# Graph attention layer on Trainium2: where the unused gather places point

## The chip, the cores and the metric

The kernel runs on one core of one Trainium2 chip (trn2). The metric is the device time of one execution in microseconds (us). TensorE is called PE here, its weight loads PEld, VectorE DVE, ScalarE ACT, GpSimd POOL and SyncE SP; ACTq, SPq and POOLq are their DMA queues.

## The reference

A relation-aware graph attention layer with a residual and a layer norm. There are N = 6250 nodes of 256 channels, E = 100000 edges sorted by their destination, and R = 5 relations with 4 heads of 64 channels:

```python
Q = (einsum('nc,rch->rnh', x, Wq) + bq).reshape(R, N, HEADS, OUT)   # K and V alike
q_i, k_j, v_j = Q[edge_type, dst], K[edge_type, src], V[edge_type, src]
score = sum(q_i * k_j, axis=-1) * scale
seg = dst * R + edge_type
e = exp(score - segment_max(score, seg)[seg]);  alpha = e / segment_sum(e, seg)[seg]
out = segment_sum(v_j * alpha, dst) + bias
return layernorm(x + out)
```

## The kernel before

**Three stages.** From 0 to about 322 us DVE sorts the edges while PE projects the queries: each of NT = 49 tiles of 128 nodes gives QC = 3 chunks of queries, NOQ = 147 in all, which go to the table `q_tab` in HBM (31250 rows of 256 float32, 1 KB each; the row of node n and relation r is 5n + r). From 322 to about 810 us PE projects keys and values, 5 chunks of 512 columns a tile, 245 in all (line 633), into four PSUM banks. DVE adds the bias to each (line 1168) and writes it to one of two stage buffers; the ACT queue stores a whole tile of 1280 KB from there to `kv_tab` (line 796; 31250 rows of 512 float32, 2 KB each). From about 811 to 1920 us the edges are worked off in 208 steps of four tiles of 128 edge places. Then come the sums across pieces and the layer norm.

**Slots of nodes.** Besides the 100000 edges, the sorted list has one extra entry for each of 49 x 128 = 6272 node numbers, so that every node occurs. `real` is 1 for an edge and 0 for such a slot. The 831 tiles in use (USED) hold 106368 places, so 6368 of them, 7.66 a tile, are no edges; the last 96 are padding. `kvidx` has for every place the row of `kv_tab` that POOL gathers (line 468), one indirect DMA for each tile of 128 places, 256 KB; the row is `lof * real` (line 1029), where `lof` is relation times N plus source. `nodef` is the node of the place. What a slot fetches is not used further.

**The block list.** Edges with the same destination and relation share one query row. While PE projects keys and values, POOL gathers query rows in sorted order from `q_tab` (line 450) and SP writes them to a second table, `q_seg` (line 506). The sorted edges lie in 128 rows of F = 1024 places, one a partition, of which ROWS = 104 are in use; the distinct segments of each row are packed in blocks of RB = 32. `seg_tab` in HBM holds their q_tab rows, 32 blocks for each row. There are BLK x 128 = 9 x 128 = 1152 places for blocks. Function `ranks` (lines 1095 to 1144) works out which block of `seg_tab` each place takes and writes it to `blk_i` (line 1143), for partition p and column b the place 128 b + p; POOL reads the blocks into `seg_list` by nine indirect DMAs (line 438), and then issues NQ = 288 gathers, each of 128 rows of 1 KB: gather j takes column j of `seg_list`, which is entry j mod 32 of the 128 blocks of column j div 32.

With the inputs of the reference, counted on the host, 984 of the 1152 places hold a block: columns 0 to 6 wholly, column 7 in partitions 0 to 87, column 8 in none. A place without a block takes a row of `seg_tab` of partition 127, where every entry is 0. So the gathers j = 224 to 255 fetch row 0 of `q_tab` in 40 of 128 partitions, and j = 256 to 287 in all 128. The blocks in use hold 30022 segments; their other 1466 entries are 0 as well, in both kernels.

**Order and rings.** A gather of query rows writes one of PQ = 13 buffers and waits until the write to `q_seg` from that buffer 13 gathers before has landed; from j = 73 on it also waits for a number of evicted chunks (function `done_chunks`, EASE = 72). The eviction of the first chunk of a tile waits until the store from its stage buffer two tiles before has landed (line 1166). PE waits for the eviction four chunks before. The first gather of `kv_tab` waits for all of these writes. In the third stage POOL runs up to KL = 5 steps of gathers ahead of DVE's products (line 1201), and a ring of KS = 22 steps ties it to PE's sums (line 697).

**Where DVE works out the indices.** After the sort DVE runs `ranks` in one piece, then steps 0 to 3 of `indices` (line 1029 is step 3), and only then starts to evict (lines 1162 and 1168). The wrapper `c(...)` waits for each instruction before the next is issued; `c.go(...)` doesn't.

Of the kernel before, what the change touches and what calls it, by code (L numbers as in the profile page):

```python
# [5 lines left out]
P = 128  # L6


def gnn_kernel(nc, x, src, dst, etype, Wq, bq, Wk, bk, Wv, bv, bias, out):
    f32, i32, u16, bf16 = mybir.dt.float32, mybir.dt.int32, mybir.dt.uint16, mybir.dt.bfloat16  # L10
    ALU, ACT, AX = mybir.AluOpType, mybir.ActivationFunctionType, mybir.AxisListType
# [23 lines left out]
    F = 1024  # L35
# [35 lines left out]
    RB = 32  # L71
    ROWS = -(-USED // FH)
# [73 lines left out]
    with ctx:  # L146
        def sb(name, shape, dt=f32):
            return ctx.enter_context(nc.sbuf_tensor(name, shape, dt))

        def sem(name):  # L150
            return ctx.enter_context(nc.semaphore(name))
# [5 lines left out]
        part_f = sb("part_f", [P, 1])  # L157
        kvidx = sb("kvidx", [P, TT], i32)
# [20 lines left out]
        def cut(words):  # L179
            nonlocal top  # L180
            top += words
            assert top <= REGION, top
            return region[:, top - words:top]
# [13 lines left out]
        lof, real, segi_w, is_head, is_tail = cut(TT), cut(TT), cut(TT), cut(TT), cut(TT)  # L197
# [15 lines left out]
        seg_list, blk_i = cut(NQ).bitcast(i32), cut(BLK).bitcast(i32)  # L213
# [3 lines left out]
        nodef = other[:, 0:TT]  # L217
# [10 lines left out]
        nblk, b32 = st0[:, 2 * F + 2 * P:2 * F + 2 * P + 1], st0[:, 2 * F + 2 * P + 1:2 * F + 2 * P + 2]  # L228
        cmp32 = st0[:, 2 * F + 2 * P + 8:2 * F + 2 * P + 8 + RB]
        below = st0[:, 0:BLK * P].rearrange("p (b n) -> p b n", b=BLK)  # L230
        bval, bcnt, bmax = (pqf[:, 3 * F + 16 * u:3 * F + 16 * u + BLK] for u in range(3))
# [66 lines left out]
        s_ranks, s_nblk, s_prefix, s_blocks = sem("s_ranks"), sem("s_nblk"), sem("s_prefix"), sem("s_blocks")  # L298
# [654 lines left out]
        def _(dve):  # L953
            c = Chain(dve, s_dve)
# [20 lines left out]
                                                op0=ALU.mult, op1=ALU.add))  # L975
# [34 lines left out]
            def indices(step):  # L1010
# [12 lines left out]
                if step == 2:  # L1023
# [2 lines left out]
                    c(nc.vector.scalar_tensor_tensor(out=lof[:], in0=nrel[:], scalar=-float(SRCS - N), in1=lof[:],  # L1026
                                                     op0=ALU.mult, op1=ALU.add))
                if step == 3:
                    c(nc.vector.tensor_tensor(kvidx[:], lof[:], real[:], ALU.mult))
                if step == 4:  # L1030

                    nc.vector.tensor_scalar(nodef[:], nodef[:], float(P * NT), None, ALU.min).then_inc(s_node, 1)
# [4 lines left out]
                if step == 7:  # L1037
                    dve.wait_ge(s_cast, 1)
                    c.go(nc.vector.scalar_tensor_tensor(out=rel[:, 0:512], in0=bank[5][:], scalar=float(N0MAX),
                                                        in1=nodef[:, 0:512], op0=ALU.min, op1=ALU.subtract))  # L1040
                    c.go(nc.vector.scalar_tensor_tensor(out=rel[:, 512:TT], in0=bank[6][:, 0:TT - 512],
                                                        scalar=float(N0MAX), in1=nodef[:, 512:TT], op0=ALU.min,
                                                        op1=ALU.subtract))
# [18 lines left out]
                if step == 10:  # L1062
# [4 lines left out]
                                                     in1=nrel[:, 0:NCK], op0=ALU.add, op1=ALU.mult))  # L1067
# [9 lines left out]
                if step == 13:  # L1077

                    c(nc.vector.scalar_tensor_tensor(out=nrel[:], in0=rel[:], scalar=1.0, in1=real[:],
                                                     op0=ALU.subtract, op1=ALU.mult))  # L1080
                    c(nc.vector.tensor_scalar(nrel[:], nrel[:], -1.0, -1.0, ALU.mult, ALU.add))
                if step == 14:

                    c(nc.vector.scalar_tensor_tensor(out=nrel[:], in0=is_head[:], scalar=float(P + 2), in1=nrel[:],
                                                     op0=ALU.mult, op1=ALU.add))
                    c(nc.vector.scalar_tensor_tensor(out=nrel[:], in0=is_tail[:], scalar=float(P + 3), in1=nrel[:],
                                                     op0=ALU.mult, op1=ALU.add))
# [7 lines left out]
            def ranks():  # L1095
# [16 lines left out]
                                               in0=cum.rearrange("p (f n) -> p f n", n=P), scalar=1.0,  # L1112
                                               in1=base_l.unsqueeze(2).broadcast_to([P, FH, P]), op0=ALU.subtract,
                                               op1=ALU.subtract).then_inc(s_ranks, 1)
                c(nc.vector.scalar_tensor_tensor(out=word[:], in0=seg_r[:], scalar=10, in1=place[:],
                                                 op0=ALU.logical_shift_left, op1=ALU.bitwise_or))
# [3 lines left out]
                for k in range(10):  # L1120
# [8 lines left out]
                                                 op0=ALU.mult, op1=ALU.add))  # L1129
# [10 lines left out]
                c(nc.vector.tensor_tensor(bval[:], bval[:], bmax[:], ALU.subtract))  # L1140
                c(nc.vector.scalar_tensor_tensor(out=bval[:], in0=bcnt[:], scalar=float(F // RB), in1=bval[:],
                                                 op0=ALU.mult, op1=ALU.add))
                nc.vector.tensor_scalar(blk_i[:], bval[:], float(F // RB), float(P * F // RB - 1), ALU.subtract, ALU.min
                                        ).then_inc(s_blocks, 1)

            for e in range(len(NET)):
                sort_entry(e)
            dve.wait_ge(s_sort, len(NET))
            ranks()
            for step in range(4):  # L1150
                indices(step)
            dve.wait_ge(s_b, 16 * 2 * R)
            dve.wait_ge(s_bq, 16 * R)
            for o in range(OS, NO):
                t, c0, w = chunk(o)
                n = nodes(t)
                if OA <= o < NOQ:
                    if o % QC == 0:
                        dve.wait_ge(s_qout[t % 2], 16 * (t // 2))
                    dve.wait_ge(s_proj, o + 1)  # L1160
                    q0 = c0 - 2 * R * C
                    nc.vector.tensor_tensor(stage_q[0:n, t % 2, q0:q0 + w], bank[o % 4][0:n, 0:w],
                                            bq_sb[0:n, q0:q0 + w], ALU.add).then_inc(s_evD, 1)
                if o >= NOQ:
                    if t >= 2 and c0 == 0:
                        dve.wait_ge(s_kvout[t % 2], 16 * (t // 2))
                    dve.wait_ge(s_proj, o + 1)
                    nc.vector.tensor_tensor(stage[0:n, t % 2, c0:c0 + w], bank[o % 4][0:n, 0:w],  # L1168
                                            b_sb[0:n, c0:c0 + w], ALU.add).then_inc(s_evD, 1)
                if o >= Z + 4:  # L1170
                    indices(o - Z)
# [258 lines left out]
```

## Time and profile before

| | us |
|---|---|
| median of 3 runs | 2065.13 (2061.58 to 2067.93) |
| profiled execution, its own time | 2069.55 |
| its span, first to last instruction | 2067.7 |
| DVE busy | 1617.8 (78%) |
| PE busy | 1689.1 (82%) |
| POOL busy | 1150.7 (56%) |

The profiled execution is taken by the hardware profiler. Busy time leaves out register, branch, semaphore and DMA-issuing instructions, but counts POOL's work on an indirect DMA. In the slices, each digit is the busy share of one fortieth of the span (51.7 us), in tenths, 9 for 90% or more; PEclk is the granted PE clock in tenths of full speed, DMA the busy share of the 16 DMA engines, and GB/s what they moved. A DMA's landing time runs from its issue until its data is there. The granted clock has two levels, 2.4 GHz (1.00) and 1.2 GHz (0.50).

### The profile page before, as it was taken

What the parts mean: (1) busy time and instruction counts of PE and PEld (TensorE: products, weight loads), DVE (VectorE), ACT (ScalarE), POOL (GpSimd) and SP (SyncE); (2) the same over time, 40 slices, a digit from 0 to 9 for tenths busy, and PEclk for the clock granted to TensorE, in tenths of its full rate; (3) what the DMA queues carried; (4) which work ended last, traced back from release to release, by engine and by line L of the source; (5) the groups of instructions that cost most, each with busy time, mean ns of one, the idle gap of its engine ahead of it and who ended that gap; (6) DMA issues with size and microseconds to landing.
All of it is one profiled execution on the core that took longest, in us unless ns stands there. A gap on an engine that the chain in (4) does not pass through costs nothing.

```text
span 2067.7 us, 33198 instructions
## 1 busy us (share of the span) xinstructions
PE 1689.1 (82%) x7565; PEld 1132.7 (55%) x7565; DVE 1617.8 (78%) x4144; ACT 1045.3 (51%) x4107; POOL 1150.7 (56%) x1215
## 2 busy tenths in 40 slices
PE   6999999999999497578877878778877888777545
PEld 2444444444444143466766766667666776666543
DVE  7988897354443143789999999999999999999648
ACT  1223230200000000078888888878888788878845
POOL 2000005777777302777777777777777777776104
PEclk9999999999999798789999999999999999999879
DMA  6333336999999965999999999999999999999006
GB/s 211 123 122 122 117 132 203 317 359 364 364 362 320 175 198 204 349 325 322 330 328 323 313 335 319 326 312 315 334 334 313 306 320 335 331 317 308 24 22 207
DMA packets 339496, 555.34 MB, mean 269 GB/s; under 512 B 44045, under 2 KB 238831, under 8 KB 339298
## 3 DMA queue, kind: packets, MB, share of 16 engines
q0 software_dynamic: 80880, 256.60, 38.2%
q1 hardware_dynamic: 222180, 228.67, 33.9%
q10 hardware_dynamic: 36238, 67.94, 9.0%
q8 instruction: 61, 1.00, 0.2%
q14 instruction: 137, 1.12, 0.2%
HBM read 412.09 MB, written 140.94 MB: 267 GB/s over the span
## 4 chain that ended last, share of the span: by engine, by line
DVE 40%; PE 29%; issue 17%; DMA 6%; POOL 4%; DVEq 3%; ACT 1%; SPq 0%; ACTq 0%; POOLq 0%
PE sums L633 23%; DVE region L1258 6%; DVE region L996 6%; DVE region L1201 5%; POOL region L468 4%; DVE region L1190 4%; DVE acc L1284 3%; DMA kv_tab<-region 3%; PE pairs L709 3%; PE sums L697 2%; DVE region L1267 2%; DMA region<-kv_tab,kvidx 2%; DVEq L1275 2%; DVE region L1212 1%; DVE region L1250 1%
## 5 line engine op out<-in xcount | busy, mean ns | idle before, releaser
L468 POOL DMA_INDIRECT region<-kv_tab,kvidx x831 | 818.3, 985 | 360.3 <-issue 213.0
L633 PE MATMUL sums<-region,acc 128*128 128x512 f32 (+2 forms) x1568 | 683.4, 582 | 32.0 <-DVE region L1168 31.7
L881 ACT ACTIVATE region<-region 128x64 f32<-128x64 f32 x2496 | 694.6, 352 | 0.0
L709 PE MATMUL pairs<-region 128*128 128x256 f32 x1664 | 450.7, 418 | 175.8 <-DVE region L1201 157.6
L633 PEld LDWEIGHTS sums<-region,acc 128*128 128x128 f32 (+1 forms) x1568 | 286.4, 191 | 336.4 <-issue 292.2
L709 PEld LDWEIGHTS pairs<-region 128*128 128x128 f32 x1664 | 324.1, 205 | 252.1 <-issue 197.5
L697 PE MATMUL sums<-region 128*128 128x131 f32 x3328 | 433.2, 284 | 27.9 <-issue 24.5
L697 PEld LDWEIGHTS sums<-region 128*128 128x128 f32 x3328 | 412.7, 197 | 57.7 <-issue 44.8
L1168 DVE TENSOR_TENSOR region<-sums,region 128x512 f32<-128x512 f32 (+1 forms) x245 | 168.3, 691 | 286.9 <-PE sums L633 239.4
L450 POOL DMA_INDIRECT region<-q_tab,region x288 | 274.5, 953 | 122.0 <-issue 58.9
L899 ACT COPY acc<-sums 128x256 f32 x832 | 305.8, 368 | 29.7 <-PE sums L697 28.3
L1201 DVE TENSOR_TENSOR region<-region,pairs 128x512 f32<-128x512 f32 x416 | 278.5, 677 | 32.6 <-DMA region<-kv_tab,kvidx 21.4
L1207 DVE TENSOR_REDUCE region<-region 128x16 f32<-128x1024 f32 x208 | 252.3, 1213 | 0.6 <-issue 0.2
L868 ACT COPY region<-bank 128x128 f32<-128x128 f32 x26 | 6.9, 265 | 460.8 <-PE bank L679 460.6
L1258 DVE TENSOR_SCALAR region<-iota_f,nrel 128x131 f32<-128x131 f32 x832 | 195.9, 313 | 10.3 <-PE sums L697 10.3
L996 DVE TENSOR_TENSOR region<-region 128x512 f32<-128x512 f32 x292 | 189.0, 689 | 5.1
L787 ACT COPY region<-sums 128x512 f32<-128x512 f32 x138 | 71.0, 514 | 210.2 <-PE sums L633 210.2
L1284 DVE TENSOR_TENSOR acc<-acc,region 128x2 f32 x832 | 130.9, 157 | 31.6 <-ACT region L907 10.8
L430 POOL DMA_DIRECT2D rel_tab<-region x1 | 0.8, 766 | 245.7 <-DVE region L1111 245.7
L1190 DVE TENSOR_SCALAR region<-region,part_f 128x512 f32<-128x512 bf16 x208 | 102.3, 492 | 10.2 <-DMA region<-rel_tab 10.2
L477 POOL TENSOR_TENSOR region<-region 128x256 f32<-128x256 f32 (+1 forms) x49 | 35.4, 731 | 113.8 <-DMA region<-in_x 113.5
L1267 DVE TENSOR_TENSOR region<-region 128x256 f32<-128x256 f32 x208 | 87.0, 418 | 0.0
(239 smaller groups left out, 943.6 us busy)
## 6 DMA issues: line engine op xcount, KB each, us to landing
region<-q_seg SPq DMA_DIRECT2D x832, 128.0 KB
kv_tab<-region ACTq DMA_DIRECT2D x48, 1280.0 KB, 7.8
q_seg<-region SPq DMA_DIRECT2D x288, 128.0 KB, 5.7
q_tab<-region SPq DMA_DIRECT2D x48, 640.0 KB, 3.3
region<-rel_tab SPq DMA_DIRECT2D x208, 128.0 KB, 5.2
region<-kv_tab,kvidx POOLq DMA_INDIRECT x831
region<-in_x SPq DMA_DIRECT2D x96, 128.0 KB, 3.2
out<-region SPq DMA_DIRECT2D x48, 128.0 KB, 2.5
```

What stands on the lines that cost most here:

```text
L450: pool.indirect_dma_start(pq[:, j % PQ, :], None, q_tab, bass.IndirectOffsetOnAxis(ap=seg_list[:, j:j + 1], axis=0)).then_inc(s_pq[j % PQ] ...
L468: pool.indirect_dma_start(ring_row[:, a:a + 2 * C], None, kv_tab, bass.IndirectOffsetOnAxis(ap=kvidx[:, t:t + 1], axis=0)).then_inc(s_got[ ...
L633: done = nc.tensor.matmul(bank[o % 4][0:n, 0:w], acc[:, k, t * P:t * P + n], w_sb[:, k, :, :].rearrange("p u c -> p (u c)")[:, c0:c0 + w], ...
L697: done = nc.tensor.matmul(bank[i][:, h * W:(h + 1) * W], ring_v[:, i, spot(q), h * P:(h + 1) * P], oneh[:, q % 2, i, :], start=True, stop= ...
L709: done = nc.tensor.matmul(qk[:, i, :], oht[:, s % 2, i * P:(i + 1) * P], qring[:, s % QS, i, :], start=True, stop=True)
L881: done = nc.scalar.activation(ring_v[:, i, spot(q), h * D:(h + 1) * D], ring_v[:, i, spot(q), h * D:(h + 1) * D], ACT.Copy, scale=alT[:, h ...
L899: nc.scalar.copy(acc[:, :, bass.ds(at[(q % 2) * SB + i] + 1, P)], bank[i][:, 0:2 * W].rearrange("p (h n) -> p h n", h=2)[:, :, 0:P]).then_ ...
L996: nc.vector.tensor_tensor(to[:, :, half, :], one, other_half, ALU.max if half else ALU.min).then_inc(s_sort, 1)
L1201: nc.vector.tensor_tensor(prod[:, two, :], ring_k[:, two, spot(s), :], qk[:, two, :], ALU.mult).then_inc(s_mul, 1)
L1207: nc.vector.tensor_reduce(sc[:, (s // PERC) % 2, :, g:g + SB].rearrange("p h g -> p g h"), prod.rearrange("p i (h d) -> p i h d", h=H), AX ...
L1258: done = nc.vector.tensor_scalar(oneh[:, q % 2, i, :], iota_f[:, 1:W + 1], nrel[:, t:t + 1], None, ALU.is_equal)
L1284: nc.vector.tensor_tensor(acc[:, :, bass.ds(col, 1)], acc[:, :, bass.ds(col, 1)], cols[:, q % CS, i, :, 2:3], ALU.add).then_inc(s_acc, 1)
```

## The change

Three places. In step 3 of `indices` the row gathered by a slot becomes the number of its node in place of 0: kvidx = (lof - nodef) * real + nodef, two more DVE operations on 128 x 832. In `ranks` a place without a block takes a block by its partition: the first block of row p for p < 104, the second block of row p - 104 for the others. For that `blk_i` is worked out by six small DVE operations instead of one. `b32` and `bcnt` are buffers that are free at that point.

```diff
                 if step == 3:
-                    c(nc.vector.tensor_tensor(kvidx[:], lof[:], real[:], ALU.mult))
+                    c(nc.vector.tensor_tensor(lof[:], lof[:], nodef[:], ALU.subtract))
+                    c(nc.vector.tensor_tensor(lof[:], lof[:], real[:], ALU.mult))
+                    c(nc.vector.tensor_tensor(kvidx[:], lof[:], nodef[:], ALU.add))
...
-                nc.vector.tensor_scalar(blk_i[:], bval[:], float(F // RB), float(P * F // RB - 1), ALU.subtract, ALU.min
-                                        ).then_inc(s_blocks, 1)
+
+                per = F // RB
+                c(nc.vector.tensor_scalar(b32[:], part_f[:, 0:1], float(ROWS), 1.0 - ROWS * per, ALU.is_ge, ALU.mult))
+                c(nc.vector.scalar_tensor_tensor(out=b32[:], in0=part_f[:, 0:1], scalar=float(per), in1=b32[:],
+                                                 op0=ALU.mult, op1=ALU.add))
+                c.go(nc.vector.tensor_scalar(bcnt[:], bval[:], float((ROWS + 1) * per), None, ALU.is_lt))
+                c(nc.vector.tensor_scalar(bval[:], bval[:], float(per), b32[:, 0:1], ALU.subtract, ALU.subtract))
+                c(nc.vector.tensor_tensor(bval[:], bval[:], bcnt[:], ALU.mult))
+                nc.vector.tensor_scalar(blk_i[:], bval[:], b32[:, 0:1], None, ALU.add).then_inc(s_blocks, 1)
```

## Rows read from the trace of the kernel before

**Rows 1.** The profile's page: the span in 40 slices.

```profile
PE   6999999999999497578877878778877888777545
DVE  7988897354443143789999999999999999999648
PEclk9999999999999798789999999999999999999879
DMA  6333336999999965999999999999999999999006
GB/s 211 123 122 122 117 132 203 317 359 364 364 362 320 175 198 204 349 325 322 330 328 323 313 335 319 326 312 315 334 334 313 306 320 335 331 317 308 24 22 207
```

**Rows 2.** Chain of waits that ended last, 650 to 910 us: start, length, what.

```profile
649.98 8.60 PE sums L633 x20
658.60 0.70 DVE region L1168
659.32 28.55 DMA kv_tab<-region
687.90 0.70 DVE region L1168
688.65 3.80 PE sums L633 x4
692.47 0.70 DVE region L1168
693.19 30.77 DMA kv_tab<-region
723.98 0.70 DVE region L1168
724.72 82.33 PE sums L633 x184
807.07 0.70 DVE region L1168
```

**Rows 3.** Busy time by stretch: length, PE, PEld, DVE, ACT, POOL (x), PEclk, DMA share, GB/s.

```profile
424.83:658.58 233.75, 233.75 (x545) 103.89 (x546) 95.09 (x138) 0.00 (x0) 176.76 (x188) 1.00 1.03 363
658.58:688.65 30.07, 15.44 (x37) 6.49 (x36) 4.80 (x8) 0.00 (x0) 12.20 (x13) 0.80 1.02 189
706.30:724.72 18.42, 2.13 (x5) 0.58 (x4) 0.74 (x2) 0.00 (x0) 2.83 (x3) 0.61 1.02 167
```

**Rows 4.** POOL's instructions in order of time: start, length, what, idle before and releaser.

```profile
656.01 0.94 POOL L450 DMA_INDIRECT region<-q_tab,region  x1 [0.30 <-DVE region L1168]
...
658.51 0.95 POOL L450 DMA_INDIRECT region<-q_tab,region  x1 [0.30 <-DMA q_seg<-region]
659.76 0.95 POOL L450 DMA_INDIRECT region<-q_tab,region  x1 [0.30 <-issue]
...
675.97 0.94 POOL L450 DMA_INDIRECT region<-q_tab,region  x1 [5.12 <-DMA q_seg<-region]
...
728.37 0.95 POOL L450 DMA_INDIRECT region<-q_tab,region  x1 [0.30 <-issue]
```

**Rows 5.** Line 796 (stores to kv_tab), landing: started 500 to 550, then 615 to 655 us.

```profile
DMA to landing us min/median/max: 7.2/7.6/8.1
DMA to landing us min/median/max: 8.7/8.8/8.9
```

**Rows 6.** Line 450 (query gathers), landing: 500 to 550, 615 to 655, 658.6 to 690 us.

```profile
DMA to landing us min/median/max: 3.7/5.1/6.7
DMA to landing us min/median/max: 3.9/5.9/7.0
DMA to landing us min/median/max: 6.0/11.7/15.7
```

**Rows 7.** Line 1168 after 659.5 us: count, min/median/max ns, first and last start.

```profile
L1168 DVE TENSOR_TENSOR region<-sums,region x65: 680/691/693, 661.6 to 807.1; 128x512 f32<-128x512 f32 x60, 106x512 f32<-106x512 f32 x5
```

**Rows 8.** DVE's instructions in order of time, 315 to 322 us.

```profile
315.25 0.17 DVE L1140 TENSOR_TENSOR region<-region 128x9 f32<-128x9 f32 x1
315.45 0.17 DVE L1141 SCALAR_TENSOR_TENSOR region<-region 128x9 f32<-128x9 f32 x1
315.66 0.17 DVE L1143 TENSOR_SCALAR region<-region 128x9 int32<-128x9 f32 x1
315.74 0.59 DVE L1015 TENSOR_SCALAR region<-region 128x832 f32<-128x832 uint16 x1
...
319.63 1.02 DVE L1026 SCALAR_TENSOR_TENSOR region<-nrel,region 128x832 f32<-128x832 f32 x1
320.69 1.03 DVE L1029 TENSOR_TENSOR kvidx<-region 128x832 int32<-128x832 f32 x1
321.75 2.22 DVE L1162 TENSOR_TENSOR region<-sums,region 128x512 f32<-128x512 f32 x4
```

**Rows 9.** PE's instructions in order of time, 322 us.

```profile
322.49 12.29 PE L633 MATMUL sums<-region,acc 128*128 128x512 f32 x32 [0.23 <-DVE region L1162]
```

**Rows 10.** DVE's waits, 811 to 1920 us: total, times, longest.

```profile
DVE region L1201 <- DMA region<-kv_tab,kvidx: 21.4, 17, 3.0
DVE region L1201 <- issue: 11.2, 24, 0.5
```

**Rows 11.** Busy time 905 to 1907 us, columns as in group 3.

```profile
905.00:1907.00 1002.00, 796.31 (x4850) 680.17 (x4849) 967.59 (x2923) 820.53 (x3415) 746.37 (x757) 0.96 0.97 323
```

## The prediction

> **What bounds the kernel now.** I read the page's slices first, then the chain of waits, then busy time by stretch, and last the instructions and landing times of the lines that the chain names. The slices [rows 1] show three stages. DVE is the fullest engine at the start (the sort), PE from about slice 8, DVE again from about slice 19. One thing breaks the pattern: in slice 13, counted from 0, the DMA engines are as busy as before, but what they move falls from 360 to 175 GB/s, and PE's digit drops to 4. The chain [rows 2] shows what that costs. Up to 658.6 us it is PE's matmuls back to back. Then it runs twice through a store to kv_tab, 28.55 and 30.77 us long, and only from 724.72 us through matmuls again. A store of the same size lands in 7.6 us earlier on [rows 5]. By stretch [rows 3], PE is busy for all of 233.75 us before, for 15.44 of 30.07 us in the first of the two waits, and for 2.13 of 18.42 us at the end of the second; the DMA share stays at 1.02 while the rate falls from 363 to 189 and 167 GB/s.
>
> **What the engines do in that time.** POOL's instructions give the date [rows 4]. The last of the 288 query gathers starts at 728.37 us; 34 stand from 656.01 us on in that view, so gather j = 256, the first one that reads row 0 in all 128 partitions, is the one at 658.51 us. The slow store starts 0.8 us later. Stores, q_seg writes and gathers have not changed in kind or size at that point; only the row that is read has. Gathers land after a median of 11.7 us instead of 5.1 [rows 6], POOL finds its ring of 13 buffers full and waits 5.12 us for one [rows 4], and the stores on another queue land late with them. Column 7, where 40 of 128 partitions read row 0, is the mild form: gathers 5.9 us, stores 8.8 us [rows 5, 6], and PE doesn't stop. So row 0 gives out a limited flow: 32 gathers of 128 KB in the 69.9 us from 658.51 to 728.37 us are 60 GB/s, an estimate of that limit. Column 7 asks for 40 KB every 1.25 us (the spacing in rows 4), 33 GB/s, under it.
>
> The Trainium skill, DMA: Bandwidth & Descriptors, section Issuing engines are not separate DMA queues, states that DMAs of all issuing engines run on the same 16 DMA engines and interleave. The trace agrees, with its store of 28.55 us beside gathers of another queue.
>
> **Part 1: the places of the block list, what is removed.** With 128 different rows in the gathers 256 to 287 I expect them to run as the ones before. POOL issues them 1.25 us apart, so the last starts at 658.5 + 31 x 1.25 = 697 us, and PE goes on without a stop. One chunk takes 233.75 / 545 x 4 = 1.716 us [rows 3] (four matmul records a chunk). After the eviction at 658.60 us there are 65 more [rows 7], so the last one would start at 658.60 + 65 x 1.716 = 770.1 us instead of 807.07 us [rows 2]: **-37.0 us**. This holds the two stalls as well as the half clock after them: the four matmuls at 688.65 us take 3.80 us, 0.95 us each for 0.43 before. What is late next is nothing but PE itself, at its full clock. The cover is thin, though: a stage buffer is wanted again 8.6 us after its store starts (5 chunks x 1.716), the stores took 8.8 us in column 7 [rows 5], and four banks of PSUM give PE a few us beyond that. Bounds of the gain: 37.0 from above by PE's rate; from below see the first rival.
>
> **Part 2: six small operations for one.** The last small operations of ranks are 0.20 us apart, an operation that isn't waited for costs 0.08 us (315.66 to 315.74) [rows 8]. Five are added, four waited for: 4 x 0.20 + 0.08 = **+0.9 us**. Behind them on DVE stand the index steps and the first evictions; POOL waits for blk_i and starts its gathers 0.9 us later, which is covered, as they end more than 70 us before the projections do.
>
> **Part 3: two operations on 128 x 832.** From one to the next it is 1.06 us (319.63, 320.69, 321.75) [rows 8]: **+2.1 us**. These are not covered. DVE's first eviction at 321.75 us ends PE's wait at 322.49 us [rows 9]: PE had filled its four banks and stood for 0.23 us. Everything from there to 658 us is PE at its rate or DVE's index steps, so the 3.0 us of parts 2 and 3 go into the end one for one. The bounds are 2.5 (some wait further on eats a part) and 3.5.
>
> **Part 4: the slots' rows in kv_tab.** The trace shows no gather of kv_tab without its 7.66 rows of 128 that are row 0, so this is bounded. A tile of 128 takes about 1002 / 757 = 1.32 us [rows 11], so row 0 is asked for 7.66 x 2 KB, about 12 GB/s: well under column 7's 33 GB/s, which cost a gather 0.8 us of landing and no engine anything. From above, DVE waits 21.4 + 11.2 = 32.6 us in all at the products that need these gathers [rows 10]; more can't come back. From below, DVE is busy 967.59 of 1002 us [rows 11], and earlier data that DVE isn't waiting for is worth nothing, 0; rows near each other could also be 1 or 2 us worse. I take 12/33 of 0.8 us, 0.3 us, at some three landings that stand on the chain while the ring fills: **-1.0 us**, nearest the column 7 row.
>
> **The sum.** -37.0 + 0.9 + 2.1 - 1.0 = -35.0 us. Against the profiled execution, 2069.55 - 35.0 = 2034.6 us. That execution was 4.4 us above the median of the runs, so against the median 2065.13 - 35.0 = 2030.1 us, which I round to 2030.
>
> **Rival 1: the bus is full without the hot row too.** The DMA engines are at 1.03 before the stall [rows 3] and the stores have under 1 us to spare. If the four or five stores from 658 to 697 us land after 15 us instead of 8.8, DVE waits over 6 us each, PE some 3, so about 15 us of the 37 stay: 2030 + 15 = 2045. For it speaks the 8.8 us; against it, that this itself comes with row 0 in column 7 and that 233.75 us went by at the same load without a stop. 8 in 100.
>
> **Rival 2: the third stage gains too.** If reads of row 0 hold up the DMA engines at 12 GB/s already, half of the 32.6 us [rows 10] returns: 2030 - 16 + 1 = 2015. For it: the DMA share is 0.97 at only 323 GB/s there [rows 11], against 363 before. Against it: DVE is busy 96.6% of that stretch, and column 7 stood 33 GB/s. 7 in 100.
>
> **Rival 3: row 0 isn't the cause, or the places still lead to it.** Then the stall stays and only the operations are added: 2065.1 + 3.0 = 2068, 0.15% above. Against it is the date of the stall to 1 us. 3 in 100.
>
> **Rival 4, slower.** The new rows lie at an even distance: partition p reads the start of row p of 104, so neighbours are about 31250 / 104 = 300 rows of 1 KB, some 308 KB, apart, and the gathers of columns 7 and 8 all have that pattern, while in use neighbouring places are some 30 rows apart. If such rows shared one part of the memory and were given out at half row 0's rate, the stall would be twice as long: 2065.1 + 3.0 + 37.0 = 2105. It decides from the point where gathers take longer than the 11.7 us of row 0 [rows 6]. No row shows this distance; that the starts scatter by several rows speaks against it, as does that each address is another. 3 in 100.
>
> The Trainium skill, DMA: Bandwidth & Descriptors, section Latency and other measured facts, has a rule against this change: copies whose partitions lie 512 KiB to 8 MiB apart, by powers of two, ran at 207 down to 103 GB/s, and a pitch padded by 4 KiB at full rate. No run here shows such a pitch; 308 KB with scatter is no power of two, so by the page too the full rate is likelier, and its 103 GB/s would be a case of this rival.
>
> **From the cases to the numbers.** The forecast has 79 in 100: 2030, with its own range 2022 to 2038 (the median's spread of 3 us, the 2.5 to 3.5, two or three us in stage three). I stretch it to 2018 below and 2043 above to take in the near parts of rivals 1 and 2. A measurement of this kernel can tell about 0.3%, 6 us, from no change. Faster: 79 + 8 + 7 = 94. Same: 3. Slower: 3.
>
> **What would show it.** Right: in the changed profile DMA GB/s stays near 360 to about 700 us, the chain has no store to kv_tab of over 10 us, the last eviction at line 1168 starts near 773 us, gathers of line 450 land after about 5 to 6 us to the end with 1.25 us between them, and the first eviction starts near 324.8 us. From the last eviction to the end it takes as long as before, to within 3 us. Wrong: a stall at gather 256 that remains (rival 3 or 4), stores of 12 us and more from 658 to 697 us (rival 1), or fewer waits at line 1201 and a third stage over 10 us shorter (rival 2).

## The result and the profile after

| | before | after |
|---|---|---|
| median, us | 2066.02 (4 runs) | 2041.23 (4 runs, 2034.3 to 2043.67) |
| profiled execution, us | 2069.55 | 2043.67 |

The ratio is 0.9881, 95% interval 0.9855 to 0.9907: 24.8 us by the medians. A second comparison on one chip (experiment 1) gave 0.986, interval 0.984 to 0.9881, which is 29 us. I had said 2030 and 35 us. The measured time lies in the stated range of 2018 to 2043, but above the 2022 to 2038 that the forecast had for itself; only the stretch for the near parts of rivals 1 and 2 takes it in.

The slices of the page after, which answer to [rows 1]:

```profile
PE   5999999999999995687788877788777887788645
DVE  7988897454443344799999999999999999999548
PEclk9999999999999997899999999999999999989668
DMA  6333344999999948999999999999999999998006
GB/s 214 124 124 109 124 141 160 313 350 364 364 362 363 339 154 292 339 318 329 320 316 320 318 333 311 320 320 321 334 309 321 320 326 329 324 306 291 24 22 210
```

Slice 13 (664 to 715 us here) moves 339 GB/s where it moved 175, and PE's digit stays at 9 up to slice 14. In the chain of waits that ended last, one piece of PE's matmuls runs through to the last eviction, in place of all that stands before it in [rows 2], and the store behind that eviction is short (its longest pieces up to the first gather of kv_tab):

```profile
599.83 175.12 PE sums L633 x408
776.04 1.96 DMA kv_tab<-region
```

Busy time of the same stretches as in [rows 3] (length, PE, PEld, DVE, ACT, POOL, PEclk, DMA share, GB/s):

```profile
658.60:688.60 30.00, 30.00 (x72) 13.26 (x71) 12.06 (x18) 0.00 (x0) 22.69 (x24) 1.00 1.02 363
706.30:724.70 18.40, 18.40 (x44) 8.12 (x43) 7.59 (x11) 0.00 (x0) 0.00 (x0) 1.00 0.48 176
```

PE is busy for all of both stretches at the full clock. Landing times of the query gathers started from 658.6 to 690 us, and of the stores to kv_tab in the same time, which answer to [rows 6] and to the slow store in [rows 2]:

```profile
DMA to landing us min/median/max: 3.6/5.2/6.6
DMA to landing us min/median/max: 7.0/7.3/7.7
```

Gathers 5.2 us in place of 11.7, stores 7.3 in place of 28.55. In column 7, the stretch from 615 to 655 us, the stores now land in 7.9 us where they took 8.8 [rows 5]. POOL's last query gather starts at 701.52 us, 1.25 us after the one before it. The evictions of keys and values, with the line number of the changed kernel [rows 7]:

```profile
L1177 DVE TENSOR_TENSOR region<-sums,region x67: 680/690/692, 661.7 to 775.0; 128x512 f32<-128x512 f32 x62, 106x512 f32<-106x512 f32 x5
```

The last one starts at 775.0 us instead of 807.1.

The places without a block now have neighbours some 308 KB apart. The gathers above show no harm from that. The Trainium skill, DMA: Bandwidth & Descriptors, section Latency and other measured facts, gives lower rates for row pitches of 512 KiB to 8 MiB by powers of two, and for one of 4 MiB plus 192 bytes. No run here has such a pitch; 308 KB isn't among them, and it ran at 363 GB/s.

**What the operations cost.** DVE in order of time, the answer to [rows 8]:

```profile
315.66 0.15 DVE L1147 TENSOR_SCALAR region<-part_f 128x1 f32<-128x1 f32 x1
315.85 0.16 DVE L1148 SCALAR_TENSOR_TENSOR region<-part_f,region 128x1 f32<-128x1 f32 x1
316.04 0.17 DVE L1150 TENSOR_SCALAR region<-region 128x9 f32<-128x9 f32 x1
316.12 0.22 DVE L1151 TENSOR_SCALAR region<-region 128x9 f32<-128x9 f32 x1
316.38 0.17 DVE L1152 TENSOR_TENSOR region<-region 128x9 f32<-128x9 f32 x1
316.58 0.23 DVE L1153 TENSOR_SCALAR region<-region 128x9 int32<-128x9 f32 x1
316.72 0.58 DVE L1015 TENSOR_SCALAR region<-region 128x832 f32<-128x832 uint16 x1
...
321.67 1.02 DVE L1029 TENSOR_TENSOR region<-region 128x832 f32<-128x832 f32 x1
322.73 1.03 DVE L1030 TENSOR_TENSOR region<-region 128x832 f32<-128x832 f32 x1
323.79 1.02 DVE L1031 TENSOR_TENSOR kvidx<-region 128x832 int32<-128x832 f32 x1
324.85 1.29 DVE L1171 TENSOR_TENSOR region<-sums,region 128x512 f32<-128x512 f32 x2
```

Line 1015 starts 0.98 us later than before (forecast 0.9), the two large operations add 2.12 (2.1), and the first eviction comes 3.10 us later. PE's instruction behind that wait, the answer to [rows 9], and the busy time around it:

```profile
325.60 13.99 PE L633 MATMUL sums<-region,acc 128*128 128x512 f32 x32 [3.31 <-DVE region L1171]
```

```profile
325.50:329.00 3.50, 3.40 (x6) 1.80 (x7) 2.05 (x5) 0.00 (x0) 2.58 (x4) 0.65 0.53 194
329.00:339.50 10.50, 10.50 (x28) 5.12 (x28) 4.70 (x9) 0.00 (x0) 4.20 (x5) 0.95 0.41 126
```

The same 32 matmuls that took 12.29 us take 13.99. PE now stands for 3.31 us instead of 0.23, and the granted clock behind it is 0.65 of full over 3.5 us, a mix of its two levels 1.2 and 2.4 GHz. These 1.7 us stand in no term of my sum.

**Where the time went**, from profile to profile:

| stretch | before | after | difference |
|---|---|---|---|
| to PE's matmul behind the first eviction | 322.49 | 325.60 | +3.1 |
| from there to the first gather of kv_tab | 488.9 (to 811.4) | 453.7 (to 779.3) | -35.2 |
| first to last gather of kv_tab | 1095.5 (to 1906.9) | 1101.5 (to 1880.8) | +6.0 |
| from there to the end of the span | 160.8 | 161.1 | +0.3 |

The -35.2 us hold the +1.7 of the clock, so the stall itself gave back 36.9. The third stage took 6 us more. DVE's waits for its gathers, the answer to [rows 10]:

```profile
DVE region L1210 <- DMA region<-kv_tab,kvidx: 24.5, 21, 2.3
DVE region L1210 <- issue: 11.1, 24, 0.5
```

They are 24.5 us, not fewer than the 21.4 of before. From the last eviction to the end it is 1266.9 us where it was 1260.6, 6.3 us more, and I had allowed 3. Was that a price of the slots' rows, or chance?

### The profile page after: what moved, and what is told of

Same layout as the page of the kernel before. It is cut to its first block, busy times and chain, and to the rows that moved or that the text cites. A ratio compares the mean times of both kernels' runs of the same rounds, so it can differ in the third digit from the quotient of the medians.

```text
span 2041.9 us, 33205 instructions
## 1 busy us (share of the span) xinstructions
PE 1692.2 (83%) x7565; PEld 1136.7 (56%) x7565; DVE 1619.3 (79%) x4151; ACT 1045.8 (51%) x4107; POOL 1152.7 (56%) x1215
## 4 chain that ended last, share of the span: by engine, by line
DVE 35%; PE 33%; issue 16%; POOL 8%; DMA 4%; DVEq 2%; ACT 1%; SPq 0%; ACTq 0%; POOLq 0%
PE sums L633 24%; POOL region L468 8%; DVE region L996 6%; DVE region L1267 5%; DVE region L1210 4%; PE pairs L709 4%; DVE region L1199 3%; PE sums L697 3%; DMA region<-kv_tab,kvidx 3%; DVE acc L1293 3%; DVE region L1276 2%; DVEq L1284 1%; DVE region L1221 1%; DVE region L1400 1%; DVE region L1403 1%
## 5 line engine op out<-in xcount | busy, mean ns | idle before, releaser
L697 PE MATMUL sums<-region 128*128 128x131 f32 x3328 | 438.5, 286 | 28.1 <-issue 24.5
L697 PEld LDWEIGHTS sums<-region 128*128 128x128 f32 x3328 | 417.1, 199 | 60.2 <-issue 52.2
L1210 DVE TENSOR_TENSOR region<-region,pairs 128x512 f32<-128x512 f32 x416 | 278.3, 675 | 36.5 <-DMA region<-kv_tab,kvidx 24.5
```

Of the source, the lines that this page charges most:

```text
L697: done = nc.tensor.matmul(bank[i][:, h * W:(h + 1) * W], ring_v[:, i, spot(q), h * P:(h + 1) * P], oneh[:, q % 2, i, :], start=True, stop= ...
L1210: nc.vector.tensor_tensor(prod[:, two, :], ring_k[:, two, spot(s), :], qk[:, two, :], ALU.mult).then_inc(s_mul, 1)
```

## The experiments

**First batch: the parts, each against the kernel before, on one chip.** Experiment 1 is the changed kernel once more, with no edit.

> The changed kernel once more, beside the kernel before and the three parts on the same chip. About 25 us faster (the first runs), of which 32 us are gained by the time the first gather of kv_tab starts and some 6 us given back after it. If the 6 us are chance, this profile's third stage (first gather of kv_tab to last) comes out at 1095 to 1100 us like before's 1095.5; if they belong to the change, at 1101 us again.

Experiment 2 keeps the block list's part and leaves kvidx as before:

```diff
-                    c(nc.vector.tensor_tensor(lof[:], lof[:], nodef[:], ALU.subtract))
-                    c(nc.vector.tensor_tensor(lof[:], lof[:], real[:], ALU.mult))
-                    c(nc.vector.tensor_tensor(kvidx[:], lof[:], nodef[:], ALU.add))
+                    c(nc.vector.tensor_tensor(kvidx[:], lof[:], real[:], ALU.mult))
```

> The places of the block list alone; kvidx as before. Theory (the whole gain is the hot row 0 in q_tab, the slots' part costs 2.1 us of DVE and gives nothing): 27 to 32 us faster than before, about 2 us better than the whole change or more if PE's clock doesn't fall at 322 us. Rival (the slots' part is worth something in the third stage): no better than the whole change. Rival (the slots' rows cost the third stage 6 us): about 8 us better than the whole change.

Experiment 3 is the reverse: the three lines for kvidx in the kernel before, whose block list stays.

> The slots' rows alone; the block list as before, so both long stores to kv_tab stay. Theory: 2.1 us of DVE before the first eviction, perhaps 1 to 2 us of half clock with it, nothing gained: 2 to 4 us slower than before. Rival (third stage gains from it): faster than before. Rival (it costs the third stage 6 us): 8 to 10 us slower.

Experiment 4 has all the operations of the change, with constants by which every index is the one of before:

```diff
-                    c(nc.vector.tensor_tensor(lof[:], lof[:], real[:], ALU.mult))
-                    c(nc.vector.tensor_tensor(kvidx[:], lof[:], nodef[:], ALU.add))
+                    c(nc.vector.tensor_tensor(lof[:], lof[:], nodef[:], ALU.add))
+                    c(nc.vector.tensor_tensor(kvidx[:], lof[:], real[:], ALU.mult))
...
-                c(nc.vector.tensor_scalar(b32[:], part_f[:, 0:1], float(ROWS), 1.0 - ROWS * per, ALU.is_ge, ALU.mult))
-                c(nc.vector.scalar_tensor_tensor(out=b32[:], in0=part_f[:, 0:1], scalar=float(per), in1=b32[:],
+                c(nc.vector.tensor_scalar(b32[:], part_f[:, 0:1], 0.0, float(P * per - 1), ALU.mult, ALU.add))
+                c(nc.vector.scalar_tensor_tensor(out=b32[:], in0=part_f[:, 0:1], scalar=0.0, in1=b32[:],
```

> All the added DVE operations, but with constants by which every index is the one of before (unused places row 0, slots row 0). Theory: the stall stays, first eviction 3.1 us later, PE's stop before it is 3.3 us long and the clock is halved for some us after it: 3 to 5 us slower than before. If it is equal to before, something covers the operations.

Measured. In the rows of experiments 1 to 4 the ratio is to the kernel before on the same chip (median 2068.53 us, 23 runs) with its interval; that of the first profile of after is the result's, from four runs of each. "To first gather" runs from PE's matmul behind the first eviction, "third stage" from first to last gather of kv_tab; both are from the one profile of each kernel.

| kernel | ratio | PE's stop before it, us | to first gather, us | third stage, us |
|---|---|---|---|---|
| before (first profile) | 1 | 0.23 | 488.9 | 1095.5 |
| after (first profile) | 0.9881 | 3.31 | 453.7 | 1101.5 |
| 1, after again | 0.986 (0.984 to 0.9881) | 3.34 | 453.7 | 1097.5 |
| 2, blocks only | 0.9859 (0.9843 to 0.9876) | 1.23 | 452.0 | 1102.0 |
| 3, slots only | 1.001 (0.9997 to 1.0023) | 2.35 | 481.7 | 1097.9 |
| 4, operations only | 1.0015 (0.9999 to 1.0032) | 3.35 | 480.8 | 1098.7 |

The whole gain is the block list's: with it alone the kernel takes 2040.35 us by the median, beside 2038.72 for the whole change; without its rows, slots only takes 2071.03 and operations only 2071.82. I had expected these two 2 to 4 and 3 to 5 us above the kernel before. By the medians they are, with 2.5 and 3.3 us, but both intervals still hold no change. The third stage takes 1095.5, 1102.0 and 1098.7 us with row 0 in the slots and 1101.5, 1097.5 and 1097.9 with their own rows: means of 1098.7 and 1099.0. The changed kernel alone gives 1101.5 and 1097.5, so the 6 us between the first two profiles are within chance, and no gain or loss from the slots' part shows; one of 1 or 2 us wouldn't. Its two operations bring 2.1 us of DVE. I had expected blocks only about 2 us or more ahead of the whole change, and it isn't, but the intervals are some 4 us wide to each side.

The clock shows between the kernels. The chain's matmuls behind the stop in blocks only and in slots only (PE in order of time):

```profile
324.41 12.29 PE L633 MATMUL sums<-region,acc 128*128 128x512 f32 x32 [1.23 <-DVE region L1169]
```

```profile
329.27 13.98 PE L633 MATMUL sums<-region,acc 128*128 128x512 f32 x32 [2.35 <-DVE region L1164]
```

After the stop of 1.23 us the granted clock is 1.00 over 3.5 us, after the one of 2.35 us it is 0.68; that is also the 1.7 us between 453.7 and 452.0.

The stall itself has no fixed size. Without it the stretch to the first gather is 452.0 us, or 453.7 with the slow clock. By that it was 36.9 us in the first profile of before, 28.0 in slots only and 27.1 in operations only. The chain of operations only shows it in three pieces instead of two:

```profile
664.66 24.30 DMA kv_tab<-region
688.98 0.70 DVE region L1177
689.72 3.80 PE sums L633 x4
693.54 0.70 DVE region L1177
694.26 19.56 DMA kv_tab<-region
...
719.14 17.58 DMA kv_tab<-region
```

No store in it is as long as the 28.55 and 30.77 us of [rows 2], and behind each the clock is at 0.50 for the next four matmuls.

Whole executions say what is lost on average. Operations only has every operation of the changed kernel and differs from it in the indices alone. Its 12 runs have a mean of 2070.8 us, the 5 of the changed kernel on that chip 2040.4: the rows are worth 30 us, 4 more or less by the spread of the runs. The kernel before and blocks only are 28.4 us apart (2068.7 and 2040.3), and blocks only carries PE's stop of 1.23 us. So the 36.9 us of the first profile lie above the average.

**Second batch: is it one row?** This and the third batch ran on two other chips, where every kernel took some 15% longer than in the first, the kernel before 2385.94 and 2377.98 us (medians of 7), most of it in the third stage. The cause isn't known; comparisons are made within a batch. Experiment 5 is the kernel before, with no edit.

> The kernel before once more, for the size of the stall. From the store of rel_tab at line 430 to the first gather of kv_tab the first profile took 551.6 us; the changed kernel takes 519.5 us in both of its profiles, ops_only (same rows as before, DVE operations added) 542.4. If the stall is a fixed size at given timing, 551 to 552 again; if it depends on how the transfers happen to fall, anything from 540 to 555.

It took 640.9 us there, so this batch doesn't answer that question. (The 542.4 us given for operations only should be 546.6.)

Experiment 6 gives all places without a block one and the same block:

```diff
-                c(nc.vector.tensor_scalar(b32[:], part_f[:, 0:1], float(ROWS), 1.0 - ROWS * per, ALU.is_ge, ALU.mult))
-                c(nc.vector.scalar_tensor_tensor(out=b32[:], in0=part_f[:, 0:1], scalar=float(per), in1=b32[:],
+                c(nc.vector.tensor_scalar(b32[:], part_f[:, 0:1], 0.0, float(50 * per), ALU.mult, ALU.add))
+                c(nc.vector.scalar_tensor_tensor(out=b32[:], in0=part_f[:, 0:1], scalar=0.0, in1=b32[:],
```

> Places without a block all take the first block of row 50, a block in use: gather j from 256 on reads one row in all 128 partitions, but the next gather another row. Row 0 itself isn't read there. Theory (a single row gives out a limited flow, whichever it is): the stall is there, stores to kv_tab of 15 us and more, 540 to 555 us from line 430 to the first gather of kv_tab. Rival (row 0 of q_tab is special, or only the same row over many gathers is slow): as the changed kernel, 519.5 us and gathers that land in 5 to 6 us.

Experiment 7 gives them two:

```diff
-                c(nc.vector.tensor_scalar(b32[:], part_f[:, 0:1], float(ROWS), 1.0 - ROWS * per, ALU.is_ge, ALU.mult))
-                c(nc.vector.scalar_tensor_tensor(out=b32[:], in0=part_f[:, 0:1], scalar=float(per), in1=b32[:],
-                                                 op0=ALU.mult, op1=ALU.add))
+                c(nc.vector.tensor_scalar(b32[:], part_f[:, 0:1], 64.0, float(60 * per), ALU.is_ge, ALU.mult))
+                c(nc.vector.tensor_scalar(b32[:], b32[:], 1.0, float(20 * per), ALU.mult, ALU.add))
```

> The same with two blocks, row 20 for partitions 0 to 63 and row 80 for the others, so each gather reads two rows 64 times. If the limit is one of each row (some 60 GB/s by the estimate), two rows give 120 GB/s against 102 GB/s that are asked for: little or no stall, 519 to 525 us, stores below 12 us. If it is not per row, the stall stays at 540 us or more.

Times: 2387.86 us for the kernel before, 2356.91 for one block, 2361.43 for two (one run each). From PE's matmul behind the first eviction to the first gather of kv_tab: 578.2, 546.7 and 547.6 us. Both kernels with blocks have the stop of 3.3 us and the 1.7 us of clock behind it, so the stall of this profile of the kernel before is 33.2 us. Busy time from 720 to 760 us, in the gathers of column 8, of the kernel before and of one block:

```profile
720.00:760.00 40.00, 29.76 (x64) 12.80 (x63) 10.67 (x16) 0.00 (x0) 17.88 (x20) 0.87 1.01 197
```

```profile
720.00:760.00 40.00, 40.00 (x95) 17.69 (x94) 16.15 (x24) 0.00 (x0) 26.01 (x28) 1.00 0.98 316
```

My theory lost here: each of these gathers reads a single row in all 128 partitions, and there is no stall. Either row 0 is special, or it takes the same row in many gathers one after another. Two blocks could then tell nothing more.

**Third batch: one row through all gathers.** Experiment 8 changes only what the entries of partitions 104 to 127 of seg_tab hold, in the kernel before; a place without a block takes partition 127's, so row 30000 stands in for row 0:

```diff
+                c(nc.vector.tensor_scalar(b32[:], part_f[:, 0:1], float(ROWS - 1), 0.0, ALU.subtract, ALU.max))
+                c(nc.vector.tensor_scalar(b32[:], b32[:], 1250.0, None, ALU.mult))
+                c(nc.vector.tensor_scalar(place[:], place[:], b32[:, 0:1], None, ALU.add))
```

> The kernel before, but every place without a block leads to row 30000 of q_tab instead of row 0, the same one in all 32 gathers of column 8. One_block (one row in a gather, another in the next) had no stall, so what is open is whether the cause is row 0 itself or one row read through many gathers. Theory A (one row for a long time, whichever): the stall is there, stores to kv_tab of 15 us and more, DVE waits over 30 us for them at line 1168. Theory B (row 0 is special, also because other gathers in flight read it): no store above 12 us, time as blocks_only.

Experiment 9 has the same three lines in blocks only, and takes the entries of partition 104 or 105:

```diff
+                c(nc.vector.tensor_scalar(b32[:], part_f[:, 0:1], 64.0, float(per), ALU.is_ge, ALU.mult))
+                c(nc.vector.tensor_scalar(b32[:], b32[:], 1.0, float(ROWS * per), ALU.mult, ALU.add))
```

> Places without a block lead to row 1250 of q_tab in partitions 0 to 63 and to row 2500 in the others, through all 32 gathers of column 8; 51 GB/s from each row at POOL's spacing. Under theory A with a limit for each row of some 60 GB/s: no stall, or a small one (DVE waits below 10 us for stores to kv_tab). If the limit is not per row: over 30 us of waits. Under theory B: no stall in either.

Experiment 10 is blocks only, with row 0 left in half the partitions:

```diff
-                c(nc.vector.tensor_scalar(b32[:], part_f[:, 0:1], float(ROWS), 1.0 - ROWS * per, ALU.is_ge, ALU.mult))
+                c(nc.vector.tensor_scalar(b32[:], part_f[:, 0:1], 64.0, float(P * per - 1), ALU.is_ge, ALU.mult))
...
+                c(nc.vector.tensor_scalar(b32[:], b32[:], float(P * per - 1), None, ALU.min))
```

> Places without a block lead to row 0 in partitions 64 to 127 and to blocks by their partition in the others: the gathers of column 8 read row 0 64 times, 51 GB/s at POOL's spacing against the 60 that I estimated as the limit. Expected: no stall or a small one, stores to kv_tab of 8.8 to 12 us. If the limit is lower or the cost goes with the number of reads of row 0: half of the kernel before's stall, stores of 15 us or more.

Times, one run each beside the 2377.98 us of before: one row 2373.62, two rows 2346.18, half zero 2352.03. To the first gather: 579.8, 549.5 and 550.7 us, so one row stalls for some 30 us. DVE's waits at its evictions for stores to kv_tab (total, times, longest) in one row, two rows and half zero:

```profile
DVE region L1171 <- DMA kv_tab<-region: 42.9, 5, 16.6
```

```profile
DVE region L1177 <- DMA kv_tab<-region: 13.3, 6, 5.1
```

```profile
DVE region L1176 <- DMA kv_tab<-region: 16.7, 5, 5.0
```

And busy time from 720 to 760 us in one row and two rows:

```profile
720.00:760.00 40.00, 27.60 (x60) 11.96 (x59) 10.11 (x16) 0.00 (x0) 17.80 (x19) 0.83 0.98 186
```

```profile
720.00:760.00 40.00, 40.00 (x95) 17.72 (x94) 16.66 (x25) 0.00 (x0) 24.63 (x27) 1.00 0.98 315
```

Row 30000 stalls as row 0 does, 186 GB/s at a DMA share of 0.98, so row 0 isn't special. Half the reads on the same row, be it two rows or row 0 beside others, and DVE waits up to 5 us at a time, while PE stands for 0.25 us (half zero) or not at all (two rows). In experiment 12, on the same chip and with no row shared by all the unused places, the trace names no store that DVE waits for (3.4 us of its waits there have no cause named). POOL's gathers were 1.46 us apart in two rows (36 from 715.1 to 766.2 us), so each row gave 64 KB in 1.46 us, 45 GB/s; they are 1.46 us apart in experiment 12 too, so the shared rows didn't set that pace. One row read alone gave, by the estimate of the prediction, 60 GB/s in the first profile, 57 in operations only and slots only, and 61 and 62 in the kernel before and one row of these batches, where POOL waited for evictions rather than for its ring. Two rows together gave 90, more than any of them, so the limit goes by the row and not by the gather.

Why one block doesn't stall stays open. At 1.25 to 1.5 us between gathers that land after 5 (the first batch; the others show no landing times), three or four are under way together, each on another row in that kernel; that the reads so spread over some rows at any moment fits, but no run shows it.

**A version with the index steps moved.** Experiments 11 and 12 are one kernel in two batches: the block list's part alone, its constant (`fall`, a buffer of its own) worked out while DVE waits for the edges, and steps 0 to 3 of indices put behind evictions instead of ahead of them all.

```diff
+            c.join()
+            c(nc.vector.tensor_scalar(fall[:], part_f[:, 0:1], float(ROWS), 1.0 - ROWS * (F // RB), ALU.is_ge, ALU.mult))
+            c(nc.vector.scalar_tensor_tensor(out=fall[:], in0=part_f[:, 0:1], scalar=float(F // RB), in1=fall[:],
+                                             op0=ALU.mult, op1=ALU.add))
             dve.wait_ge(s_edges, 96)
...
-            for step in range(4):
-                indices(step)
...
-                if o >= Z + 4:
+                if o >= Z:
                     indices(o - Z)
```

> Block list part of the change without the slots' part, with its two constants worked out while DVE waits for the edges, and steps 0 to 3 of indices moved behind the first evictions, between those of four chunks. Theory: PE's stop before the first eviction at 322 us and the halved clock behind it go (4.8 us in the changed kernel), so 514 to 515 us from line 430 to the first gather of kv_tab, and 4 to 6 us faster than the changed kernel, 1.5 to 1.7% faster than before. Rival (evictions and index steps together are too much for DVE): 516 us and more, no better than blocks_only.

> The version with late index steps again, on another chip I hope: beside blocks_only's 0.9859 and the whole change's 0.986 it should stand at 0.983 to 0.985 of the kernel before. From the store of rel_tab to the first gather of kv_tab 513 to 516 us (whole change 519.5, blocks_only 515.7), PE without a stop at 322 us. If this is no better than blocks_only, what it gives goes lost in the third stage's spread of some 6 us.

PE in order of time, in experiment 12:

```profile
317.28 4.46 PE L634 MATMUL sums<-region,acc 128*128 128x512 f32 x12
321.76 12.21 PE L634 MATMUL sums<-region,acc 128*128 128x512 f32 x32
```

The stop in front of these 32 matmuls is gone, but there is another one right behind them, in experiment 11 and then in 12:

```profile
337.54 1.13 PE L591 MATMUL pairs<-region 128*128 128x512 f32 x2 [2.01 <-DVE region L1037]
```

```profile
335.98 1.90 PE L591 MATMUL pairs<-region 128*128 128x512 f32 x2 [2.01 <-DVE region L1037]
```

Line 591 needs step 4 of the indices (line 1037). DVE has steps 0 to 3 ahead of it as before, only between evictions: step 4 starts 18.1 us after PE's group of 12 matmuls in both executions, in blocks only 17.1. PE stands for 2.01 us; behind that the clock is 0.56 from 336.0 to 339.9 us in experiment 12 and stays at 1.00 in experiment 11. From the start of the group of 12 matmuls (317.28 us above) to that of the next group of 12 (339.97 us) it takes 22.7 us, in experiment 11 it takes 21.0. The same stretch takes 19.2 us in the first profile of before, 20.2 in blocks only and 24.0 in the changed kernel. So of the 4.8 us the move wins back 3.0 in one execution and 1.3 in the other, and against blocks only it wins nothing.

The rest of the record fits. From the store of rel_tab to the first gather of kv_tab I had expected 514 to 515 and 513 to 516 us by the first batch's measure; in these slower batches it is 610.9 beside 612.5 for one block, and 615.9 beside 614.3 for two rows. The ratios to the kernel before are 0.9871 (0.9849 to 0.9894) and 0.9866 (0.9843 to 0.9889): faster than before, but not the 0.983 to 0.985 expected, and not to be told from the whole change's 0.986 and 0.9881. In the second batch it took 2354.39 us where one block, which has the added operations of the block list and of the slots, took 2356.91.

These batches have one more thing in the way. Between about 385 and 465 us PE is at half clock (0.50) in the kernel before too, busy for 20.4 of the 80 us: it stands for up to 13.1 us at a time before the transposes of line 610, which need copies of ACT, and ACT is idle most of that time as well. What holds both up the traces don't show. The version on a chip without that wait wasn't tried.

## Why the prediction was right, and where its sum was off

- **The cause and its date** were right: gather 256 starts the stall, and with other rows in it the stores land in 7.3 us and PE runs through. Experiments 1 to 4 show that nothing else in the change does it.
- **Part 1, -37.0 us**: 36.9 by the two profiles. But I took the size from one profile as if every execution had it. Operations only and slots only show 27.1 and 28.0 us, and whole executions 30, 4 more or less. This term, 3 to 11 us too large for an average execution, is most of the 6 to 10 us between my 35 and the measured 25 to 29. What makes one execution stall for 27 us and another for 37 stays open.
- **Parts 2 and 3, +3.0 us**: 3.1. What the step lacked is PE's clock. I wrote that the 3.0 us go into the end one for one, with an upper bound of 3.5; in the profile they went in with 1.7 us on top, 4.8 in all, outside the bound. The pattern stood in my own rows, in the 3.80 us for four matmuls after the long wait [rows 2]; I charged it to the stall and not to the stop that the change makes. Whole executions of operations only are 3.3 us above the kernel before by the medians and 2.1 by the means, with an interval of -0.2 to 6.6, and can't tell 3.0 from 4.8.
- **Part 4, -1.0 us**: nothing that shows. In the third stage the means are 1098.7 and 1099.0 us, and in the second batch it takes 1325.0 us (before) against 1325.2 (one block, with the slots' rows). Two profiles of the changed kernel differ by 4 us there, so 1 us is neither shown nor excluded.
- **Rival 1** (a full bus) had the nearer number, 2045, but not its mechanism: two waits of 4.1 us in all for stores to kv_tab, none that reached PE. **Rivals 2, 3 and 4** didn't come. The condition that I put to row 0, a limited flow from one row, held for row 30000 as well, but with the addition that it must be the same row in successive gathers.

The mechanism was right, but that the number came into the range is in part luck: it owes that to the stretch for rivals that didn't come.

## What to carry to other kernels

An index that stands for nothing still moves data: where many unused places share one, look for a stretch with a full DMA share and fewer GB/s, and spread them, even over a handful of rows. Count the cost of added work in front of a busy PE with the clock that its stop may take along. When steps are moved to spare one wait, look for every engine that waits for them, as PE did at line 591. And when a stall is to be removed, take its size from more than one execution.

## What the runs showed of the hardware

- Thirty-two indirect gathers of 128 reads of one 1 KB row ran at 60 GB/s of that row, with the DMA engines at a share of 1.02, and made a store of another queue nearly four times as long (28.55 us for 7.6). Four more profiles with one row gave 57 to 62 GB/s. Half of these reads, 45 GB/s from a row, cost PE 0.25 us at most and DVE 13.3 and 16.7 us of waits for stores.
- One row in all 128 partitions of a gather did PE no harm when the next gather had another one (316 GB/s, PE busy for all of 40 us).
- A stop of PE of 1.23 us left the clock at 1.00, and one of 1.40 us in experiment 8 took nothing either (12.29 us for the 32 matmuls). One of 2.35 us and those of 3.3 us cost 1.7 us, but one of 2.39 us in experiment 9 did not (12.29 us). Of two stops of 2.01 us in the moved version, one left the clock at 1.00 and the other took it to 0.56. The length alone doesn't decide there.
